# Edge attributes split into high and low parts on GpSimd ahead of the edge loop, through a table in device memory

## The reference, cut to what matters

```
edge_feat = concatenate([x[src], x[dst], edge_attr], axis=-1)    # 512 + 512 + 64
h = mish(edge_feat @ W1 + b1)
messages = mish(h @ W2 + b2)
agg = segment_sum(messages, dst)
u = mish(concatenate([x, agg]) @ W3 + b3)
y = x + u @ W4 + b4          # then a layer norm of y
```

## Time and profile before

| what | us |
|---|---|
| median of 3 runs | 1122.53 (1121.63 to 1124.40) |
| span of the profiled execution, first to last instruction | 1119.2 |
| PE busy in the span | 1066.3 (95%) |
| ACT busy | 889.8 (80%) |
| DVE busy | 863.1 (77%) |
| POOL busy | 661.0 (59%) |

### The profile page before, as it was taken

How to read it: one execution, slowest core, us unless ns; L and a number is a source line. 1 busy time by engine, 2 the same in 40 slices (tenths; PEclk the granted TensorE clock), 3 DMA queues, 4 the chain that set the end, 5 groups by cost and what they waited for, 6 DMA issues and landing times.

```text
span 1119.2 us, 18504 instructions
## 1 busy us (share of the span) xinstructions
PE 1066.3 (95%) x5756; PEld 900.7 (80%) x5757; DVE 863.1 (77%) x1506; ACT 889.8 (80%) x1122; POOL 661.0 (59%) x558
## 2 busy tenths in 40 slices
PE   3768999999999999999999999999999999999997
PEld 1226889998888888888888888888888888888796
DVE  7998435526335588888899989998988888888786
ACT  6985736525504899999999999999999999999584
POOL 6874340002156576676888888888867677660217
PEclk9969999999999999999999999999999999999999
DMA  2005720301265486666666666666666666651002
GB/s 104 8 1 138 127 76 1 123 1 57 86 216 116 104 188 140 141 130 137 139 134 136 136 139 137 132 132 143 133 140 131 138 140 135 136 127 43 1 1 92
DMA packets 61087, 121.41 MB, mean 108 GB/s; under 512 B 7851, under 2 KB 18348, under 8 KB 60918
## 3 DMA queue, kind: packets, MB, share of 16 engines
q0 software_dynamic: 38048, 87.58, 38.3%
q1 hardware_dynamic: 22998, 33.32, 8.9%
HBM read 107.82 MB, written 7.80 MB: 103 GB/s over the span
## 4 chain that ended last, share of the span: by engine, by line
PE 88%; DVE 7%; issue 2%; ACT 2%; POOL 1%; DVEq 1%; ACTq 0%; POOLq 0%
PE banks L1072 12%; PE banks L1067 12%; PE banks L1068 12%; PE banks L970 10%; PE banks L1052 7%; PE banks L1092 6%; PE banks L1046 6%; PE banks L1013 5%; PE banks L888 4%; PE banks L1034 4%; PE banks L1065 3%; PE banks L1153 2%; DVE edge_counts L1737 2%; PE banks L818 1%; DVE key_onehot L1676 1%
## 5 line engine op out<-in xcount | busy, mean ns | idle before, releaser
L701 POOL DMA_INDIRECT gather_pq<-q_table,dst x157 | 296.0, 1885 | 57.1 <-issue 47.5
L693 POOL DMA_INDIRECT gather_pq<-p_table,src x157 | 172.9, 1101 | 136.7 <-PE banks L1052 83.6
L1067 PE MATMUL banks<-w_lo,h_hi 128*128 128x512 f32 x620 | 241.6, 390 | 0.0
L1068 PE MATMUL banks<-w_hi,h_hi 128*128 128x512 f32 x620 | 241.4, 389 | 0.0
L1072 PE MATMUL banks<-w_hi,h_lo 128*128 128x512 f32 x620 | 166.2, 390 | 0.0
L1068 PEld LDWEIGHTS banks<-w_hi,h_hi 128*128 128x128 f32 x620 | 116.4, 188 | 24.9
L1072 PEld LDWEIGHTS banks<-w_hi,h_lo 128*128 128x128 f32 x620 | 116.4, 188 | 24.2
L2050 DVE SCALAR_TENSOR_TENSOR h_full<-mish_work,banks 128x512 f32<-128x512 f32 (+1 forms) x154 | 98.5, 681 | 46.5 <-ACT mish_work L1377 42.1
L1067 PEld LDWEIGHTS banks<-w_lo,h_hi 128*128 128x128 f32 x620 | 116.5, 188 | 22.0
L2075 DVE SCALAR_TENSOR_TENSOR message<-mish_work,banks 128x1024 f32<-128x1024 f32 x78 | 95.3, 1222 | 8.7 <-ACT mish_work L1401 0.7
L1365 ACT ACTIVATE mish_work<-banks 128x1024 f32<-128x1024 f32 (+1 forms) x77 | 78.6, 1021 | 26.3 <-PE banks L1052 26.2
(11 more groups left out here) (270 smaller groups left out, 2671.5 us busy)
## 6 DMA issues: line engine op xcount, KB each, us to landing
edge_attr<-in_edge_attr_t SPq DMA_DIRECT2D x79, 128.0 KB
x_nodes<-h_hi POOLq DMA_DIRECT2D x10, 256.0 KB, 13.3
x_nodes<-h_lo POOLq DMA_DIRECT2D x10, 256.0 KB, 7.9
p_table<-p_stage SPq DMA_DIRECT2D x10, 256.0 KB, 2.0
q_table<-agg_nodes SPq DMA_DIRECT2D x10, 256.0 KB
gather_pq<-p_table,src POOLq DMA_INDIRECT x157
gather_pq<-q_table,dst POOLq DMA_INDIRECT x157
x_nodes<-in_x SPq DMA_DIRECT2D x3, 768.0 KB, 6.3
```

The source lines that it names most:

```text
L693: nc.gpsimd.indirect_dma_start(GP[:, 2 * j + k, :], None, p_tab[:, :], bass.IndirectOffsetOnAxis(ap=SRC[:, 2 * s + k:2 * s + k + 1], axis= ...
L701: nc.gpsimd.indirect_dma_start(GP[:, 2 * j + k, :], None, q_tab[:, :], bass.IndirectOffsetOnAxis(ap=DST[:, 2 * s + k:2 * s + k + 1], axis= ...
L1067: pe.matmul(at, h_high(s, j)[:, c, e], W2_LO[:, c, :], start=False, stop=False)
L1068: pe.matmul(at, h_high(s, j)[:, c, e], W2_HI[:, c, :], start=False, stop=False)
```

## The change

The split is moved ahead of the edge loop. The host now gives the 64 rows once. In the stretch of the first perceptron, SyncE loads two pairs of tiles at a time into AT_RAW (128 x 256: pair 2n in partitions 0 to 63, pair 2n+1 in 64 to 127), GpSimd casts it to `edge_attr_hi` and subtracts to `edge_attr_lo`, and SyncE stores both parts of both pairs, four stores of 64 x 256, to a table `attr_parts` in device memory. That is done 40 times with two buffers. SyncE's loads of ROWS and W1 stand behind the first 20 (ATTR_BREAK). In the edge loop SyncE loads a pair's 128 x 256 ready into one of four slots of AT_R, and ScalarE's and VectorE's instructions for it are gone. TensorE waits for the load itself, once in each step. AT_RAW, AT_HI and AT_LO have memory of their own; AT_R has twice the slots.

```diff
+ATTR_BREAK = 20
...
+            def load_raw(n, j):
+                sp.dma_start(AT_RAW[:, j, :], edge_attr_t[bass.ds(2 * n, 2), :, :].rearrange("o p e -> (o p) e")).then_inc(attr_raw[j], 16)
+
+            def store_parts(n, j):
+                for done, part, rows in ((attr_hi, AT_HI, slice(0, EDGE_DIM)), (attr_lo, AT_LO, slice(EDGE_DIM, P))):
+                    sp.wait_ge(done, n + 1)
+                    for k in range(2):
+                        sp.dma_start(at_tab[bass.ds(2 * n + k, 1), rows, :].rearrange("o p e -> (o p) e"),
+                                     part[EDGE_DIM * k:EDGE_DIM * (k + 1), j, :].bitcast(F32)).then_inc(attr_stored[j], 16)
+
+            def split_pairs(first, end):
+                with sp.Fori(first // 2, end // 2) as i:
+                    for j in range(2):
+                        store_parts(2 * i + j, j)
+                        load_raw(2 * i + 2 + j, j)
+
+            for j in range(2):
+                load_raw(j, j)
+            split_pairs(0, ATTR_BREAK)
             sp.wait_ge(mm_done, MM_2)
             sp.dma_start(ROWS[:, :, :], rows.partition_broadcast(P)).then_inc(rows_in, 16)
             sp.dma_start(WA[:, :, :], w1[0:2 * DIM, :].rearrange("(k p) n -> p k n", p=P)).then_inc(w1_in, 16)
+            split_pairs(ATTR_BREAK, PAIRS // 2 - 2)
+            for j in range(2):
+                store_parts(PAIRS // 2 - 2 + j, j)
             sp.wait_ge(mm_done, MM_PQ)
...
-            def attributes(i, pairs=2):
-                for j in range(pairs):
-                    sp.wait_ge(attr_ready, 2 * i + j - 1)
-                    sp.dma_start(AT_RAW[:, j, :], edge_attr_t[bass.ds(2 * i + j, 1), :, :]
-                                 .rearrange("o p e -> (o p) e")).then_inc(attr_in[j], 16)
+            def attributes(s, j):
+                sp.dma_start(AT_R[:, j, :].bitcast(F32), at_tab[bass.ds(s, 1), :, :].rearrange("o p e -> (o p) e")).then_inc(attr_in[j], 16)
...
+            def further_attributes(s, j):
+                sp.wait_ge(z1_done, s - SLOTS + 1)
+                attributes(s, j)
...
             nc.gpsimd.memset(T1[:, :, NW:NP], 0.0).then_inc(pool_const, 1)
+
+            def attr_parts(n):
+                j = n % 2
+                pool.wait_ge(attr_raw[j], 16 * (n // 2 + 1))
+                if n >= 2:
+                    pool.wait_ge(attr_stored[j], 64 * (n // 2))
+                nc.gpsimd.tensor_copy(AT_HI[:, j, :], AT_RAW[:, j, :]).then_inc(attr_hi, 1)
+                pool.wait_ge(attr_hi, n + 1)
+                nc.gpsimd.tensor_tensor(AT_LO[:, j, :], AT_RAW[:, j, :], AT_HI[:, j, :].bitcast(F32), ALU.subtract).then_inc(attr_lo, 1)
+
+            for n in range(PAIRS // 2):
+                attr_parts(n)
 
             pool.wait_ge(bn_ready, KH + KD)
...
-                    pe.wait_ge(attr_ready, s + 1)
+                    if b == 0:
+                        pe.wait_ge(attr_in[slot], loaded)
...
-            def attr_high(s, j, loaded):
-                act.wait_ge(attr_in[j], loaded)
-                if after(s, 2):
-                    act.wait_ge(z1_done, s - 1)
-                nc.scalar.copy(AT_R[:, j, :], AT_RAW[:, j, :]).then_inc(attr_hi, 1)
...
-            def attr_rest(s, j):
-                dve.wait_ge(attr_hi, s + 1)
-                low = AT_R[EDGE_DIM:P, j, :]
-                nc.vector.tensor_tensor(low, AT_RAW[EDGE_DIM:P, j, :], low.bitcast(F32), ALU.subtract).then_inc(attr_ready, 1)
...
-        "edge_attr_t": np.concatenate([attr, attr], axis=1),
+        "edge_attr_t": attr,
```

More of the change, by code:

```diff
@@ L400, in gnn_kernel @@
         q_moved, p_stored, q_stored = sem("q_moved"), sem("p_stored"), sem("q_stored")
-        attr_in = [sem(f"attr_in{j}") for j in range(2)]
-        attr_hi, attr_ready = sem("attr_hi"), sem("attr_ready")
+        attr_raw = [sem(f"attr_raw{j}") for j in range(2)]
+        attr_stored = [sem(f"attr_stored{j}") for j in range(2)]
+        attr_in = [sem(f"attr_in{j}") for j in range(SLOTS)]
+        attr_hi, attr_lo = sem("attr_hi"), sem("attr_lo")
         z1_done, a_exp, a_sq, a_ln, a_r, h_hi, h_lo = (sem(n) for n in
@@ L514, in _ @@
             for j in range(2):
-                sp.dma_start(AT_RAW[:, j, :], edge_attr_t[j, :, :]).then_inc(attr_in[j], 16)
+                sp.wait_ge(attr_stored[j], 16 * PAIRS)
+            def attributes(s, j):
+                sp.dma_start(AT_R[:, j, :].bitcast(F32), at_tab[bass.ds(s, 1), :, :].rearrange("o p e -> (o p) e")).then_inc(attr_in[j], 16)
+            for s in range(SLOTS):
+                attributes(s, s)
             for nt in range(NT):
@@ L518, in _ @@
                 sp.dma_start(q_tab[nt * P:(nt + 1) * P, :], AGG[:, nt, :]).then_inc(q_stored, 16)
[L520 to L535 removed]
+            def further_attributes(s, j):
+                sp.wait_ge(z1_done, s - SLOTS + 1)
+                attributes(s, j)
+            sp.wait_ge(mm_done, MM_U)
+            with sp.Fori(1, 1 + KD) as i:
+                for j in range(SLOTS):
+                    further_attributes(SLOTS * i + j, j)
+                sp.dma_start(WB[:, bass.ds(i - 1, 1), :].rearrange("p o n -> p (o n)"),
+                             w3[bass.ds(DIM + (i - 1) * P, P), :]).then_inc(w3_in, 16)
+            with sp.Fori(1 + KD, EDGE_PAIRS // SLOTS) as i:
+                for j in range(SLOTS):
+                    further_attributes(SLOTS * i + j, j)
+            for s in range(EDGE_PAIRS // SLOTS * SLOTS, EDGE_PAIRS):
+                further_attributes(s, s % SLOTS)
             sp.wait_ge(z1_done, FINAL)
@@ L1422, in edge_step @@
                     log2(s - 2)
-                if live(s + 2):
-                    attr_high(s + 2, j, loaded)
                 if live(s - 2):
                     inv2(s - 2)
-            for j in range(2):
-                attr_high(j, j, 16)
             act.wait_ge(q_stored, TABLE_STORED)
@@ L1446, in _ @@
                             inv1(s)
[L1447 to L1448 removed]
             with act.Fori(1, LAST - 1) as i:
                 for j in range(2):
[L1451 removed]
+                    edge_step(2 * i + j, j)
             for s in range(2 * (LAST - 1), EDGE_PAIRS + 2):
[L1453 removed]
+                edge_step(s, s % 2)
             def u_exponential(n):
@@ L2128, in edge_step @@
                     load_range(0, i - 1)
-            for j in range(2):
-                attr_rest(j, j)
             dve.wait_ge(q_stored, TABLE_STORED)
```

31 lines of the change are left out of this document (14 added, 17 removed).

## The result

| | before | after |
|---|---|---|
| median of 4 runs | 1122.08 us | 1188.85 us |
| lowest to highest | 1119.93 to 1124.4 | 1188.17 to 1189.57 |
| span of the profiled execution | 1119.2 us | 1187.7 us |
| mean granted clock | 0.988 | 0.970 |

The changed kernel takes 1.0597 times as long (95% interval 1.0578 to 1.0616), 67 us more. The forecast was 1141.6 us, with 1168 as its upper end: the sign was right, the size was not.

What follows compares the result with a forecast made beforehand. TensorE was taken to bound the loop, and SyncE's issues the new rounds. Terms -2.6 + 18.9 + 2.5 + 0.3 = +19.1 us on the 1119.2 us span, plus 3.3 to the median, gave 1141.6 us, range 1120 to 1168.

Steps and rivals of the forecast that it cites:

- The rate of the rounds: New rounds ahead of the loop: SyncE's five issues at 0.54 us plus 0.1 make 2.8 us a round; GpSimd needs 1.1.
- rival C: Stores of 64 rows cost 3.2 to 3.7 us a round; 1160 us at 3.3, 1174 at 3.7; chance 0.18.
- The sum to the low parts of W1: Ahead of P's product: low parts ready at 293.2 against TensorE's 274.30, so 18.9 us of pure waiting.
- Queueing behind W1: Loads of rounds 22 and 23 wait behind W1's 3.3 MB, losing 6.9 us.
- W2's load: Behind the last stores, W2 lands at 296, before VectorE needs it at 297.7: covered by 1.6 us, otherwise 0 to 4.
- the clock: At the start of P, the wait brings half speed for some 5 us, costing 2.5 us, range 0 to 10.
- GpSimd beside VectorE: Between the perceptron products, GpSimd's work holds up VectorE's split of the hidden layer: 0.3 us, between 0 and 2.6.
- The entry: At the first z1, TensorE's wait for VectorE goes, 2.2 us; first steps 0.4 more; together -2.6 us.
- The edge loop: 64 us of ScalarE's and VectorE's time removed in the loop, off the bound, so 0.
- A: Issues are cheaper, up to 0.43 us each, and all rounds are hidden; only the entry's gain is left, 1119.9 us; chance 0.10.
- B: Rounds of 2.3 to 2.6 us, or no queueing behind W1: net 0 to +12, say 1131 us; chance 0.18.
- D: The loop gains by itself, as ScalarE sometimes makes TensorE late; 0.1 us a step would be 8 us; chance 0.02.

Runs made afterwards that it cites:

- the changed kernel with the loop healed: The changed kernel, whole, with VectorE's load of the range registers moved behind lo2 of the odd step and nothing else; 1169.2 us, ratio 1.0422.
- 682.4 with the loop healed: Against the loop-only kernel, VectorE's register load moved from the even step's end to the middle of the odd step; 1117.28 us, ratio 0.9957.
- loop-only kernel: The changed kernel with only the first two rounds of splitting, the loop reloading those four pairs from fixed addresses; 1138.2 us, ratio 1.0146.
- kernel before, load moved: The kernel before with VectorE's load of the range registers moved to the odd step, behind lo2; 1121.15 us, ratio 0.9998.
- the filler: The loop-only kernel with an unused 64x256 VectorE subtraction put back in the old place of the attributes' subtraction; 1118.44 us, ratio 0.9965.

## Why the prediction was wrong, step by step

- **What bounds it, and where the hole is.** Right: the question was whether 40 rounds fit into 98.7 us, and TensorE's one long wait came where the prediction had put it.
- **The rate of the rounds.** Right that SyncE's issues set it and GpSimd (0.40 and 0.73 us) has time left. The price of one issue was mis-sized: 0.54 us was taken for all five, from a 128-row issue and its register operation. Measured are 0.67 for a store of 64 rows, 0.62 for the load, 0.17 a round for the turn, and 0.1 for stretched issues. The trace of before had the better row: two issues of 64 rows in 1.19 us, the same price as now (1.15), with fixed addresses. The prediction gave that to rival C and set it aside, as standing behind a large load. That 64 rows cost more to issue is shown by the shorter issues of the runs with 128-row stores.
- **The sum to the low parts of W1.** The formula held: 187.4 + 36 x 3.57 = 315.9, and the last split ended at 317.5. In that sum the round alone accounts for 27.7 of the 29.2 us that were missing. With 3.57 the whole sum would be -2.6 + 46.6 + 2.5 + 0.3 = 46.8, 1169.3 us, and the changed kernel with the loop healed took 1169.2.
- **Queueing behind W1, W2's load, the clock, GpSimd beside VectorE.** As forecast or near it: a pause of 11.3 us on GpSimd where some 9 were said, nothing seen of W2, +2.4 us of half clock. The 0.3 us for GpSimd beside VectorE had no place in the sum: it would make TensorE reach its wait later, and the wait ends when the low parts are ready all the same.
- **The entry.** -2.1 against -2.2 for the wait. The extra 0.4 us of the first steps is in the loop's noise (683.2 us before, 682.4 with the loop healed).
- **The edge loop.** The step that failed outright. "Off the bound, so 0" was true of the engines' busy time. But VectorE is waited for once in two steps by way of a bank, and between that operation and the segment sum stands a register load that the busy counts leave out. It was hidden with 0.1 us to spare; after, it ended 0.7 us too late, in 34 pairs of steps. A changed step time was among the prediction's own signs of being wrong. It excluded a loss without looking at what taking work away does to the others' timing, and had no rival of a slower loop.
- **The rivals.** C was right in the rate and in its price (1160 to 1174 us for 3.3 to 3.7 us a round). A, B and D fell.

## What to carry to other kernels

Price a DMA issue by its own shape: on this queue a store of 64 rows took 0.14 us more to issue than one of 128, and in a chain of small transfers the number of issues is what to count. Before taking work off an engine that "is not the bound", list every wait through which the bound engine hangs on it, with the instructions that are not counted as busy, and how much each is hidden by; 0.1 us of cover is none. And when a loop slows though it does less, look for an instruction whose duration changed though nobody touched it.

## What the runs showed of the hardware

- VectorE's load of a few registers took 0.744 to 0.759 us in all forty cases without the q gathers, and 1.44 to 1.59 us (loop-only kernel, 33 cases) with a GpSimd gather, all but one of them a q gather, begun between 0.07 us before and 0.17 us after its start. Where GpSimd's last q gather was over 0.6 us before its start, and its transfers were not, it took 1.59 us (kernel before, load moved, at 785.7 us). The next operation behind it in VectorE's queue began only when it was over.
- SyncE's issue took 0.332 us for a store of 128 rows of 1 KB and 0.473 us for one of 64 rows, and 0.2 us of register work and gap stood between two with computed addresses.
- GpSimd's busy time rose by 47 us (616.0 to 663.2, the loop-only kernel without and with the filler) with 77 more VectorE subtractions of 0.42 us, 32 us in all, beside it.
